# Attention with a spiking feed-forward gate on one core: two batches per lap of the loop, eight feed-forward groups ahead of the first scores, the last batch's side work packed closer

## The reference, cut to what matters

```python
def reference(x, Wq, Wp, bp, W_fc, W_proj):        # x: (16, 1024, 256) float32
    xn = layernorm(x)
    # attention: 16 heads of 16; q, k and v are the same projection
    q = einsum('bnhd,hed->bnhe', xn by heads, Wq)
    attn = softmax(einsum('bnhe,bmhe->bhnm', q, q) * 4)
    s = (attn @ q, heads joined) @ Wp.T + bp
    # feed-forward, then a count of spikes over 5 steps of a leaky neuron
    y = square(relu(xn @ W_fc.T)) @ W_proj.T        # 256 -> 1024 -> 256
    g = silu(spike_count(y) / 5)
    return x + s * g
```

## Time and profile before

| what | value |
|---|---|
| median of three runs | 2634.41 us (2624.84 to 2635.39) |
| the profiled execution | 2632.66 us |
| its span, first to last instruction | 2629.0 us |
| mean granted TensorE clock | 0.991 |
| PE (TensorE matmul) busy | 93% |
| ACT (ScalarE) busy | 79% |
| DVE (VectorE) busy | 53% |
| POOL (GpSimd) busy | 28% |

### The profile page before, as it was taken

One profiled execution on the slowest core, in us unless ns is written; L12 is line 12 of the kernel. 1 busy time (PEld: TensorE's weight loads), 2 busy tenths in 40 slices (PEclk: granted clock), 3 DMA queues, 4 the chain that ended last, 5 costly groups with the idle time before them and its releaser, 6 DMA issues.

```text
span 2629.0 us, 53504 instructions
## 1 busy us (share of the span) xinstructions
PE 2444.8 (93%) x18180; PEld 925.6 (35%) x18180; DVE 1388.7 (53%) x2457; ACT 2074.3 (79%) x2245; POOL 726.6 (28%) x681
## 2 busy tenths in 40 slices
PE   4999999998999989999999999999999899998997
PEld 1333333333333323333333333333333233333333
DVE  5545645456454465545555554555545645445464
ACT  3888778787887878878788787887878788887785
POOL 3323313133231332312332222332313323123240
PEclk8999999999999999999999999999999999999998
DMA  3021030210302112030120302103021020301200
GB/s 120 27 64 51 17 90 9 72 43 23 92 1 82 33 38 77 1 98 17 49 66 1 98 17 64 51 17 91 8 75 40 29 86 1 90 24 42 90 1 25
DMA packets 61365, 126.02 MB, mean 48 GB/s; under 512 B 15873, under 2 KB 17154, under 8 KB 58754
## 3 DMA queue, kind: packets, MB, share of 16 engines
q1 hardware_dynamic: 61186, 123.25, 15.5%
HBM read 89.11 MB, written 34.08 MB: 47 GB/s over the span
## 4 chain that ended last, share of the span: by engine, by line
PE 71%; DVE 12%; issue 8%; ACT 7%; DMA 0%; ACTq 0%; DVEq 0%; SPq 0%; POOL 0%; POOLq 0%
PE acc L544 31%; PE aux L458 23%; PE scores L570 17%; ACT e L705 6%; DVE cnt L810 2%; DVE h_t L800 1%; DVE r L794 1%; DVE q_hi L755 1%; DVE res L847 1%; DVE acc_t L826 1%; DVE acc_t L843 1%; ACT y_sb L660 1%; DVE cnt L807 0%; DVE acc_t L841 0%; DVE scaled_t L832 0%
## 5 line engine op out<-in xcount | busy, mean ns | idle before, releaser
L705 ACT ACTIVATE e<-scores 128x1024 f32<-128x1024 f32 x2048 | 1986.1, 1024 | 515.4 <-PE scores L570 509.8
L544 PE MATMUL acc<-e,v_ones 128*32 128x512 f32 x8192 | 988.9, 600 | 1.1 <-issue 1.1
L570 PE MATMUL scores<-query_stack,key_stack 49*128 49x512 f16 x4096 | 646.8, 384 | 35.0 <-ACT e L705 16.7
L1022 POOL TENSOR_TENSOR r_squared<-r 128x512 f32<-128x512 f32 x256 | 269.4, 1052 | 914.8 <-DVE r L794 899.6
L570 PEld LDWEIGHTS scores<-query_stack,key_stack 49*128 49x128 f16 x4096 | 176.2, 93 | 700.7 <-ACT e L705 548.6
L458 PE MATMUL aux<-w_proj,h_t 128*128 128x256 f16 x3072 | 378.4, 274 | 34.6 <-DVE c_row L764 34.6
L458 PE MATMUL aux<-xn_t,w_fc 128*128 128x512 f16 x1536 | 376.9, 382 | 33.7 <-DVE h_t L800 33.7
L544 PEld LDWEIGHTS acc<-e,v_ones 128*32 128x32 f32 x8192 | 214.5, 109 | 455.0 <-issue 452.7
L458 PEld LDWEIGHTS aux<-w_proj,h_t 128*128 128x128 f16 x3072 | 282.7, 98 | 144.7 <-issue 64.1
L794 DVE TENSOR_SCALAR r<-aux 128x512 f32<-128x512 f32 x256 | 174.6, 682 | 262.8 <-PE aux L458 229.7
L1025 POOL TENSOR_TENSOR h_t<-r_squared,h_t 128x512 f16<-128x512 f32 x256 | 299.6, 1170 | 36.7
(11 more groups left out here) (68 smaller groups left out, 998.1 us busy)
## 6 DMA issues: line engine op xcount, KB each, us to landing
key_stack<-q_scratch SPq DMA_DIRECT2D x384, 64.0 KB
query_stack<-q_scratch SPq DMA_DIRECT2D x384, 64.0 KB
x_tok<-x SPq DMA_DIRECT2D x16, 1024.0 KB, 4.8
x_out<-x SPq DMA_DIRECT2D x32, 512.0 KB, 3.8
out<-x_out SPq DMA_DIRECT2D x32, 512.0 KB, 2.6
q_scratch<-q_hi SPq DMA_DIRECT2D x32, 256.0 KB
q_scratch<-q_lo SPq DMA_DIRECT2D x32, 256.0 KB
query_stack<-c_scratch SPq DMA_DIRECT2D x128, 4.0 KB
```

Source lines behind the costliest of these rows:

```text
L544: ins = nc.tensor.matmul(acc[unit % 2][STRIP * n:STRIP * (n + 1), :], v_ones[:, j, G * g + n, :], e[:, tile, n % 2, :], start=j == 0, stop ...
L570: return nc.tensor.matmul(bank, key_stack[base:base + 49, at, j * P:(j + 1) * P], query_stack[base:base + 49, at, half * HALF:(half + 1) * ...
L705: nc.scalar.activation(e[:, tile % NE, :, :], scores[tile % 2][:, :, :], ACT.Exp, scale=4.0 if exact else SCORE_SCALE).then_inc(s.exp_done, 1)
L1022: nc.gpsimd.tensor_tensor(r_squared[:, :], tile, tile, ALU.mult).then_inc(s.rsq_set, 1)
```

## The change

`batches` runs two batches in each lap of the loop, so the 14 middle batches are 7 laps. In the first batch the first eight side groups (FC 0 to 7) are issued by TensorE ahead of its first scores, and the other engines' tasks for them stand at step 0; the rest of the side work is spread over all 64 steps. In the last batch the side work is spread over 58 steps instead of 64. The waits for the split weights move with their groups into `side`.

By the scheduler's own arithmetic, batch 0's side work in units of `COST`, for the 32 rounds, is before 1.92, 1.28, 1.92, 1.28, 1.28, 1.92, 1.28, 1.6, 1.6, 1.28, 1.6, 1.6, 1.6, 1.6, 1.28, 1.92, 1.28, 1.92, 1.28, 1.28, 1.46, 1.64, 1.46, 1.92, 1.07, 1.71, 1.6, 1.28, 1.6, 1.6, 1.6, 1.28, and after 1.28 four times, 0.96, 1.28, 1.28, 1.28, 1.6, 0.64, 1.28 six times, 1.14, 0, 0, 3.24, 1.46, 1.28, 1.07, 1.07, 1.28, 1.28, 1.28, 0.96, 1.28, 1.28, 1.28, 0.96. Y 0 begins at step 0 instead of step 13. In the last batch the rounds with 1.92 are rounds 0, 16 and 20 before, and 0, 2, 4, 6, 14, 16 and 18 after, and the last three rounds have none.

```diff
--- before.py
+++ after.py
@@ -37,6 +37,9 @@
 STEPS = UNITS * TT
 STRIP = P // G
 ROUND = 2
+LAP = 2
+LEAD = 8
+REST = 6
 BASES = (0, 64)
 ROWS = 64 + 49
 LN_EPS = 1e-5
@@ -112,21 +115,27 @@
     return own[:4] + tail + own[4:] + middle + [(0, Y, k) for k in range(2, 4)]
 
 
-def schedule(groups):
-
-
-    total = sum(COST[kind] for _, kind, _ in groups)
+def schedule(groups, first, last):
+
+
+    lead = LEAD if first else 0
+    span = STEPS - REST if last else STEPS
+    total = sum(COST[kind] for _, kind, _ in groups[lead:])
     at, step, out, done = 0.0, 0, [[] for _ in range(STEPS)], []
+    ahead = [(kind, k, part, n) for n, (_, kind, k) in enumerate(groups[:lead]) for part in range(PARTS[kind])]
     for n, (offset, kind, k) in enumerate(groups):
+        if n < lead:
+            done.append(0)
+            continue
         for part in range(PARTS[kind]):
-            step = max(step, int(at / total * STEPS))
+            step = max(step, int(at / total * span))
             if kind == PROJ:
                 step = max(step, STEPS // 2 + 6 if offset == 0 else 6)
             step = min(step, STEPS - 1)
             out[step].append((kind, k, part, n))
             at += COST[kind] / PARTS[kind]
         done.append(step)
-    return out, done
+    return ahead, out, done
 
 
 class Signals:
@@ -308,8 +317,9 @@
 
         def batches(eng, body):
             body(0, True, False)
-            with nc.Fori(1, B - 1, engines=(eng.engine,), hint_back_edge=True) as b:
-                body(b, False, False)
+            with nc.Fori(1, B - LAP, LAP, engines=(eng.engine,), hint_back_edge=True) as b:
+                for n in range(LAP):
+                    body(b + n, False, False)
             body(B - 1, False, True)
 
 
@@ -607,12 +617,25 @@
 
                 def body(b, first, last):
                     groups = batch_groups(first, last, exact)
-                    steps, _ = schedule(groups)
+                    ahead, steps, _ = schedule(groups, first, last)
                     order = ([(0, kind, k) for kind, k in prep_groups(exact)[-2:]] if first else [(b - 1, Y, 2), (b - 1, Y, 3)]) \
                         + [(b + offset, kind, k) for offset, kind, k in groups]
                     if exact:
                         wait(pe, s.exp_done, b * 128)
                         row_maxima(b)
+
+                    def side(piece):
+                        n = piece[3]
+                        if first and not exact and piece[:3] == (FC, 0, 0):
+                            pe.wait_ge(fc_split, 2)
+                        if first and not exact and piece[:3] == (Y, 0, 0):
+                            pe.wait_ge(proj_split, 2)
+                        if first and not exact and piece[:3] == (PROJ, 0, 0):
+                            pe.wait_ge(wp_split, 2)
+                        aux_part(order[n + 2][0], piece, emptied(s, order[n][1], order[n][0], order[n][2]))
+
+                    for piece in ahead:
+                        side(piece)
                     for i in range(0, STEPS, ROUND):
                         score_step(b, i)
                         for done in range(i - ROUND, i):
@@ -622,14 +645,7 @@
                                 pv(b - 1, STEPS + done)
                         score_step(b, i + 1)
                         for piece in steps[i] + steps[i + 1]:
-                            n = piece[3]
-                            if first and not exact and piece[:3] == (FC, 0, 0):
-                                pe.wait_ge(fc_split, 2)
-                            if first and not exact and piece[:3] == (Y, 0, 0):
-                                pe.wait_ge(proj_split, 2)
-                            if first and not exact and piece[:3] == (PROJ, 0, 0):
-                                pe.wait_ge(wp_split, 2)
-                            aux_part(order[n + 2][0], piece, emptied(s, order[n][1], order[n][0], order[n][2]))
+                            side(piece)
 
                 batches(pe, body)
                 for done in range(STEPS - ROUND, STEPS):
@@ -685,7 +701,7 @@ (the same line in the bodies of ScalarE, VectorE and GpSimd)
-                    _, done = schedule(groups)
+                    _, _, done = schedule(groups, first, last)
```

## The result

The changed kernel takes **2661.09 us** (median of 4 runs, 2660.97 to 2661.49) against 2633.38 for the kernel before in the same session: a ratio of **1.0112, 95% interval 1.0089 to 1.0134**. I had forecast 2641.7, with a range that ended at 2656. The change costs 27.7 us where I had 7.3.

The account below looks back on a forecast made before the run. Rounds were taken as bound by a 4.60 us floor, waiting for an exponential, not by TensorE's work. +7.0 + 2.9 - 1.5 + 0 + 1.5 - 2.6 = +7.3 gave 2641.7 us; own range 2634 to 2650, 8 in 10 2624 to 2656.

Parts of the forecast that it names:

- What bounds the kernel: Rounds of two steps: floor of 4.60 us, set by waiting for an exponential; side work up to about six matmuls is free.
- TensorE's work as the bound: Rival for the rounds: TensorE's work sets the time, so freed side work counts in full; -2.3, 2632.1 us, chance 0.10.
- Part 2: Two batches per lap: taken back edges go from 13 to 6, each free, so 0 us.
- the longer body loses the prefetch of its back edge: Rival at the loop's 6 edges: each costs at least 3.52 us; +21.1 + 7.3, 2662.8 us, chance 0.03.
- My bounds of 17.9 each way: Second body's register waits: 17.9 us saved (rival, chance 0.12) or 17.9 us added (rival, chance 0.10); 0 taken.
- +2.9 and 1.5: Costs of the two clock falls in batches 1 and 2; +2.9 us taken for one fall in the w_proj wait.
- Part 1: Eight groups ahead of batch 0's first scores, paced by GpSimd; scores start at 48.35, 3.5 us later; sum +8.4 us.
- my rival for a lead at half clock: Eight groups before the first scores run at half clock, ending at 53.7 instead of 48.35; +5.4, 2647.1 us, chance 0.08.
- The w_proj wait: Batch 0, round 0: TensorE waits from about 51.0 to 57.2 for w_proj's split; first PV at 59.25, +7.0 us.
- -1.5: Batch 0: four rounds go from nine feed-forward matmuls to six, 4 x 0.38 us saved.
- Part 3: Last batch's side work ends six steps early: +1.5 us for fuller rounds, -2.6 at the end; sum -1.1 us.
- The exit of the loop: Behind the last lap: 3.52 us of ScalarE waiting for nothing the profile shows; forecast to stay.

Follow-up runs that it names:

- lead_only: Kernel before with only the eight side groups ahead of the first scores, one batch per lap: 2641.94 us, ratio 1.0035.
- lap_only: Kernel before with only the two batches per lap, no lead and no early end: 2653.89 us, ratio 1.0076.
- act_pause2: Kernel before with a 128 x 256 ScalarE copy ahead of the exponentials of step 19 in every batch: 2654.49 us, ratio 1.0083.
- before_c_first: Kernel before with VectorE's normalisation of unit 5 two steps later, behind the squared-norm rows: 2597.12 us, ratio 0.9868.
- after_c_first: Changed kernel with VectorE's normalisation of unit 5 two steps later, behind the squared-norm rows: 2607.49 us, ratio 0.9909.
- no_lap: Changed kernel with one batch per lap, lead and early end kept: 2644.49 us, ratio 1.0048.
- act_pause: Kernel before with a 128 x 32 ScalarE copy ahead of the exponentials of step 19 in every batch: 2638.33 us, ratio 1.0025.
- lap_vector: Kernel before with two batches per lap on VectorE alone, one on the other engines: 2637.16 us, ratio 1.0013.
- rest_only: Kernel before with only the last batch's side work ending six steps early: 2630.07 us, ratio 0.9996.
- lap_tensor: Kernel before with two batches per lap on TensorE alone, one on the other engines: 2627.62 us, ratio 0.9977.

## Why the prediction was wrong, by its own steps

**What bounds the kernel: right.** In `lead_only` the rounds of batch 0 with no side work at all took 4.60 us, like those with six matmuls, and no full round of any kernel fell below it. TensorE's work as the bound of these rounds is refuted.

**Part 2 is the step that failed: "A back edge is free, so removing seven gives 0".** I read TensorE's rows across one edge and took the edge's price as fixed for all engines and any body. `lap_only` refutes it: this part alone costs 20 to 23 us, 3 of them at the edges themselves and most of the rest in clock falls, 14 instead of 2. The edge was free while ScalarE and VectorE held one batch; the likely reason is that their bodies were not brought again, which rests on the queues' bytes. I did have a rival for it, "the longer body loses the prefetch of its back edge", at 0.03 with a price of 3.52 us or more for each of 6 edges. The mechanism was close and the price wrong: 0.5 us an edge, 3 in all. That this rival's 2662.8 lies next to 2661.1 is a coincidence, since 17 of the 20 us in the loop are clock falls. My bounds of 17.9 each way stood on the register waits, which cost the same in both bodies.

**The clock falls in the loop.** I had the rows: two laps with a fall, "+2.9 and 1.5", and let my own range reach 8 us up for "more or fewer" of them. What I didn't ask is why twelve laps with the same 2.5 us wait escape (I had written 3 us, which is the wait on the side of the weight loads). `act_pause2` shows that a shift of some tenths in each lap is enough to bring the falls, and `before_c_first` and `after_c_first` that none is left without the wait. So the kernel before was in a repeating lap of 160.40 us in which the wait comes harmlessly. Why a wait is harmless at one time and not at another, no run here shows. A quantity that stands at 2 of 14 by the rhythm of a loop can go to 12 by an edit that moves a lap by tenths. It need not: `no_lap`, `act_pause` and `lap_vector` had no fall in the profiled execution. Priced so, the range would have reached 12 x 1.8 = 21 us further. The Trainium skill (TensorE: Matmul & The Clock Gate, "Terms") gives the penalty as throttled time times the share taken away. Here 4 us at a mean of 0.57 lose 1.7 us, and the 12 falls average (20.0 + 4.4 - 3.0) / 12 = 1.8: row and rule agree.

**Part 1: mechanism right, sizes off.** The groups start at 33.76 (forecast 33.25), GpSimd sets their pace, and the first scores are at 50.15 instead of 48.35. The step "I take the lead at full clock" failed: the first 30 matmuls took 9.87 us, at 0.72 in 34 to 44. In `lead_only` the same matmuls took 8.72, and the first scores came at 48.64. So this term is between my forecast and my rival for a lead at half clock, and varies. The clock in the kernel after was down before the idle time had even begun: the last four matmuls ahead of it took 2.03 us at 29.22, and 1.13 at 28.72 in the kernel before. The w_proj wait was 6.32 (forecast 6.2), w_proj's low half 3.06 (2.63). At the first PV the shift is +10.7 for my 7.0: 1.8 is the late scores, and 1.6 is the fallen clock ahead of the PV (2.74 us for the first w_proj matmuls and 1.04 for the scores, where I had 1.5 and 0.55). Behind the PV the fall cost 0.2 more, so it cost 1.8 in all and not 2.9. That the second PV is near my sum, +10.9 for 9.9, is partly luck: two errors cancel. My reason for the fall was wrong too. I had it come 4.5 us behind the last matmul, but the clock was low for nearly all of 53 to 59 (mean 0.52), behind a matmul that ended at 52.96. The term "-1.5" for rounds of nine matmuls was swamped: of the two rounds without side work, forecast at 4.60, the first took that and the second 6.29, and the crowded one behind them 10.05 for "8 to 9", as the clock fell in the second empty round. In `lead_only` there was no fall there and the three took 4.60, 4.60 and 8.41. In that kernel the whole of batch 0 costs +7.8, my sum being +8.4.

**Part 3: right in size, but the -2.1 of the table doesn't show it.** In the last batch the first three rounds behind the exit of the loop take 15.66 us in all instead of 20.42, which has nothing to do with the early end (`lap_only`, without it, has 15.29). The rounds behind them take 3.6 more, 1.9 of it in one round in which ScalarE stands idle for 1.84 us, and the stretch from the start of the last PV to the end 0.9 less. The clean pair is `no_lap` and `lead_only`: from the fourth round to the last PV 134.14 and 134.11 us, from there to the end 22.51 and 23.83. That is -1.3 where I had -1.1. `rest_only` alone can't tell such a size (0.9996, 0.9984 to 1.0009). VectorE's transpose at 2640.07 stands right behind the last PV (2638.87 + 1.06), as forecast.

**The exit of the loop** stays by my forecast; it became cheaper. The first round of the last batch takes 5.01 us instead of 6.72. It is cheap too in `lap_tensor` (4.98) and dear in `lap_vector` (7.24). Why is open.

**The chances.** Slower by over 0.5% had 0.22, almost none of it for what happened.

## What to carry to other kernels

Before a loop's body is doubled, compare its instruction bytes with what the profile's instruction queues already move: an engine whose body stays in place (few packets in spite of many laps) can start to be fetched each lap, and the engine on the critical path pays. TensorE's body could be doubled free, ScalarE's not.

Here a wait of 2.5 us on TensorE in every lap was worth removing although the clock held in most laps. Removing it gave 1.3%, and it also took away a sensitivity by which 3 us of delay became 20. When an edit changes a lap by tenths of a microsecond and the total by ten, count the laps with a low granted clock first.

## What the runs showed of the hardware that I had not expected

- Behind the same wait the clock falls or doesn't, which costs 1.4 to 3.0 us or nothing (batches without a taken edge take 160.36 us without a fall and 161.76 to 163.38 with one in the kernel after), depending on when the wait comes: behind the one that ends at 978.04 in the kernel before the clock stays at 2.4 GHz, behind the one that ends at 666.23 in the kernel after it is at 1.2.
- A 0.42 us copy on ScalarE in each lap (3 us in sum) made the kernel 20 us slower (`act_pause2`).
- Two instruction queues behave apart. One moves 2.61 MB whether TensorE's body holds one batch or two; the other moves 0.16 MB with single bodies of the other engines and 0.88 with double ones. That the first feeds TensorE, whose edges are free either way, is inferred.
- VectorE's split of 2048 columns took 3.06 us at 56.17 and 2.63 at 52.17 for the same instruction.
